# A two-layer kernel's attention: the diagonal of the scores in 32-token blocks, transposes moved to another ring, first loads spread over steps, and extra products in the first row phase

## The chip, the cores and the metric

The kernel runs on one core of a Trainium2 chip. The metric is the device time of one execution in microseconds. TensorE's granted clock has two levels here, 2.4 GHz (shown as 1.00) and 1.2 GHz (0.50).

## The reference

The whole program is two layers, each an attention followed by a mixture of experts. The change touches only the first attention: 2 sequences of 1024 tokens, 16 heads of 8 numbers each, keys and values rebuilt from a small latent.

```python
scores = jnp.einsum('bhqd,bhkd->bhqk', qh, kh) * scale
decay = jnp.exp(-LAMBDA_DECAY * TIME_STEP * jnp.abs(idx[:, None] - idx[None, :]))
scores = scores * decay[None, None, :, :]
attn = jax.nn.softmax(scores, axis=-1)
out = jnp.einsum('bhqk,bhkd->bhqd', attn, vh)
```

There is no causal mask. The decay exp(-c|i-j|) is a product of a factor of the query and a factor of the key, but a different product on each side of the diagonal: one pair of factors holds for keys before the query, another for keys after it.

## The kernel before, in words

Queries and keys are scaled with a ramp for each of the two sides ("half" 0 and 1 in the code), split into three bf16 parts, written to DRAM (parts_dram) and loaded back by load_side (L110, L113) into two big tiles, stack[0] and stack[1], four heads each. A pair of heads has two halves with a query side and a key side each, so four sides to load. Rows 72 to 74 of the stack carry the negated row maximum of each query, so that a product over 75 rows gives score minus maximum.

A head m has 8 key tiles t of 128 keys; a step is one (m, t), 256 steps in all. On TensorE one step of the main loop does, in program order:

- score_unit(m, t, 0) and (m, t, 1): scores of 128 keys against 512 queries each, into one of three PSUM banks used in turn (the score ring, NS = 3). Queries beyond the key tile use half 0, queries before it half 1, and the tile's own 128 queries use half 0. by_columns (L387) issues each product as four, one for each 32 keys, into the four column groups of the array.
- at t = 3 and 7, score_late (m, part): the 128x128 diagonal blocks of four tiles once more with half 1, 16 products of 128 columns.
- row_unit(n) for the row 15 steps ahead (LEAD): scores of 128 queries against 1024 keys into one of two row tiles (the row ring), of which DVE takes the maximum (L857).
- weigh(m, t - 2) (L501): probabilities times values, fp32, summed in out_ps; and at t = 7 and t = 1 or 2 weigh_late (L512) the same for the late blocks.
- turn_neg (L420) once in a head: a small transpose of the split maxima into the row ring. DVE copies it out (L867), and ACT's queue stores it into the stack (L627).
- turn_out (L446) once in four heads, at t = 4.

ACT does the exponentials (L641, L648). POOL zeroes the wrong triangle in each diagonal block (L768), and in the late blocks (L773), splits the maxima (L717 to L723), and in the first 12 steps prepares the second sequence's parts (L744, L752, L760). The order on each engine is the program order written here, and semaphores tie the engines together.

Before the main loop come the projections, and then 15 rows of the first phase (wide_row_unit, L412), 128 columns wide and with no scores between. After step 255 there are three tail steps, then the output copy.

## Time and the profile before

| what | value |
|---|---|
| median of 3 runs | 924.22 us (922.47 to 927.52) |
| profiled execution | 928.23 us, its span 926.8 us |
| TensorE busy | 762.0 us, 82% |
| DVE, ACT, POOL busy | 602.8, 481.3, 268.0 us |
| mean granted clock | 0.891 |

The first attention is the stretch from 0 to about 444 us. The rest of the program isn't touched.

### The profile page before, as it was taken

To read this page: it belongs to the slowest core of one execution; us is meant where nothing else is said; L and a number is where in the kernel's file an instruction comes from. 1 tells how busy PE (TensorE), PEld (TensorE's weight loads), DVE (VectorE), ACT (ScalarE), POOL (GpSimd) and SP (SyncE) were. 2 spreads that over 40 slices of the span, in tenths; PEclk is the share of its full clock that TensorE was granted. 3 is DMA by queue.
4 is the path that set the end of the run, shared out by engine and by line. 5 is a ranking of instruction groups with operands and counts; after the bars stand their busy time and mean duration, and the time that the engine had idled before them with its cause. 6 is when DMAs were issued, how large, how long until landed. Compare 5 with 4: busy or idle time off the path is not lost. (4 is left out here: it accounts for less than half of the span.)

```text
span 926.8 us, 26384 instructions
## 1 busy us (share of the span) xinstructions
PE 762.0 (82%) x10923; PEld 469.9 (51%) x10923; DVE 602.8 (65%) x1402; ACT 481.3 (52%) x966; POOL 268.0 (29%) x590
## 2 busy tenths in 40 slices
PE   6599999999999999998538949999995993128990
PEld 3246555555555555554416825666663561025770
DVE  3768888888888888883642134767677446753444
ACT  4748888787878888888214443334342322001222
POOL 2566434343334333435025522000000000015531
PEclk9759999999999999999758959999998996558995
DMA  5562411111111111000671128000000004001104
GB/s 169 164 152 101 123 55 55 53 55 47 54 55 55 54 55 44 4 4 3 190 221 41 34 80 277 2 1 1 2 1 1 1 0 137 3 6 39 39 26 145
DMA packets 40327, 59.13 MB, mean 64 GB/s; under 512 B 11108, under 2 KB 22061, under 8 KB 40208
## 3 DMA queue, kind: packets, MB, share of 16 engines
q1 hardware_dynamic: 35216, 50.09, 18.3%
q0 software_dynamic: 2304, 4.74, 2.0%
q10 hardware_dynamic: 2688, 2.61, 0.8%
q8 instruction: 87, 1.43, 0.6%
q14 instruction: 32, 0.26, 0.1%
HBM read 42.09 MB, written 15.07 MB: 62 GB/s over the span
## 5 line engine op out<-in xcount | busy, mean ns | idle before, releaser
L857 DVE CUSTOM_DVE_ANT_0 junk<-row,rest 128x1024 bf16<-128x1024 f32 x256 | 312.7, 1225 | 62.6 <-PE row L387 49.1
L641 ACT ACTIVATE prob<-score 128x512 f32<-128x512 f32 x512 | 274.3, 598 | 78.8 <-PE score L387 77.1
L387 PE MATMUL score<-stack 75*32 75x128 bf16 (+3 forms) x3840 | 179.3, 298 | 1.9 <-ACT prob L641 1.0
L501 PE MATMUL out_ps<-prob,v_aug 128*32 128x256 f32 x2048 | 156.6, 383 | 1.6 <-POOL prob L768 1.6
L387 PE MATMUL row<-stack 72*32 72x512 bf16 x1928 | 150.3, 387 | 0.7
L768 POOL TENSOR_SCALAR_AFFINE_SELECT prob<-prob 128x128 f32<-128x128 f32 x256 | 79.1, 309 | 192.5 <-ACT prob L641 187.6
L387 PEld LDWEIGHTS score<-stack 75*32 75x32 bf16 x3840 | 92.6, 97 | 65.4 <-ACT prob L641 16.7
L501 PEld LDWEIGHTS out_ps<-prob,v_aug 128*32 128x32 f32 x2048 | 62.9, 111 | 52.4 <-POOL prob L768 2.2
L1487 PE MATMUL up_ps<-rows_t,up_w 128*128 128x320 f32 (+1 forms) x192 | 62.0, 448 | 7.7 <-DVE rows_t L1699 5.0
L1773 POOL MEMSET ones<- 128x128 bf16 x2 | 0.4, 205 | 231.6 <-POOLq L1214 212.3
L387 PEld LDWEIGHTS row<-stack 72*32 72x32 bf16 x1928 | 48.6, 98 | 29.6 <-DVE top L857 5.2
L2006 PE MATMUL outs<-vm_w,mixed 128*64 128x256 f32 x512 | 61.7, 381 | 1.8 <-issue 1.8
L1786 POOL DMA_INDIRECT rows_in<-rows,owner x36 | 35.2, 978 | 69.4 <-DVE owner L1696 59.1
L2006 PEld LDWEIGHTS outs<-vm_w,mixed 128*64 128x64 f32 x512 | 41.9, 137 | 20.6 <-issue 8.1
L1798 POOL DMA_INDIRECT results<-rows_out,owner x36 | 35.8, 996 | 49.4 <-DVE rows_out L1713 41.6
L773 POOL TENSOR_SCALAR_AFFINE_SELECT prob_late<-prob_late 128x512 f32<-128x512 f32 x64 | 40.8, 637 | 26.7 <-ACT prob_late L648 26.7
L2090 ACT ACTIVATE squares<-outs 128x256 f32<-128x256 f32 x60 | 18.2, 389 | 57.4 <-PE outs L2006 57.4
L1559 ACT ACTIVATE acted<-up_ps 128x320 f32<-128x320 f32 x32 | 13.8, 437 | 61.6 <-PE up_ps L1487 42.5
L1487 PEld LDWEIGHTS up_ps<-rows_t,up_w 128*128 128x128 f32 x192 | 35.2, 206 | 19.0 <-issue 4.7
L648 ACT ACTIVATE prob_late<-score 128x512 f32<-128x512 f32 x64 | 39.0, 610 | 0.0
L2006 PEld LDWEIGHTS work<-h_t,a_w 128*64 128x64 f32 x512 | 29.1, 141 | 12.1 <-ACT mixed L2096 10.6
L1699 DVE COPY rows_t<-xturn_ps 128x256 f32<-128x256 f32 x18 | 7.6, 424 | 41.6 <-PE xturn_ps L1477 33.4
(305 smaller groups left out, 1076.1 us busy)
## 6 DMA issues: line engine op xcount, KB each, us to landing
stack<-parts_dram SPq DMA_DIRECT2D x32, 288.0 KB
stack<-parts_dram SPq DMA_DIRECT2D x96, 96.0 KB
parts_dram<-prob SPq DMA_DIRECT2D x12, 256.0 KB
parts_dram<-spare SPq DMA_DIRECT2D x12, 256.0 KB
results<-x_tok SPq DMA_DIRECT2D x12, 256.0 KB, 3.8
up_w<-in_L_ffn_w_dram SPq DMA_DIRECT2D x1, 2048.0 KB, 9.7
rows<-x_tok SPq DMA_DIRECT2D x8, 256.0 KB, 3.5
y<-results SPq DMA_DIRECT2D x8, 256.0 KB, 4.1
```

Source lines behind the costliest of these rows:

```text
L387: last = pe.matmul(out[c:c + 32, :], keys[:, c:c + 32], queries, start=True, stop=True)
L501: last = pe.matmul(out_ps[32 * c:32 * c + 32, h // 2 * (S // 4):(h // 2 + 1) * (S // 4)], v_aug[g % 3][:, t, h, :], moving[:, :, c, :], st ...
L641: act.activation(prob[:, t, w * HALF:(w + 1) * HALF], score[n % NS][:, :], ACT.Exp).then_inc(exped, 1)
L648: act.activation(prob_late[:, m % 2, w * HALF:(w + 1) * HALF], score[n % NS][:, :], ACT.Exp).then_inc(exped, 1)
L768: pool.affine_select(out=prob[:, t, at:at + P], in_=prob[:, t, at:at + P], compare_op=ALU.is_ge, fill=0.0, base=0, pattern=[[1, P]], chann ...
L773: pool.affine_select(out=prob_late[:, m % 2, of].rearrange("p (n c) -> p n c", c=P), in_=prob_late[:, m % 2, of].rearrange("p (n c) -> p n ...
L857: dve.tensor_tensor_reduce(junk[:, slot % 2, :], row[slot % 2][:, :], rest[:, S - P - t * P:2 * S - P - t * P], 1.0, LOWEST, ALU.mult, ALU ...
L1487: last = pe.matmul(up_ps[n % 2][j][:, 0:cap], w_up[:, j, e, c * P:(c + 1) * P], rows_t[:, e * cap:(e + 1) * cap], start=True, stop=True)
L1786: pool.indirect_dma_start(rows_in[:, t, :], None, rows[:, :], bass.IndirectOffsetOnAxis(owner[:, 1, t:t + 1], 0)).then_inc(r_in[t], 16)
L1798: pool.indirect_dma_start(results[:, :], bass.IndirectOffsetOnAxis(owner[:, 0, t:t + 1], 0), rows_out[:, t, :], None, bounds_check=K * T - ...
L2006: last = pe.matmul(out[c:c + HC], stationary[:, c:c + HC], moving, start=start, stop=stop)
L2090: last = act.activation(squares[:, 2 * k:2 * k + 2, :], outs[k][:, :, 0:D], ACT.Square)
```

## The change

- Diagonal blocks. In a key tile's own 128 queries, the products of each 32-key group are cut at that group's own 32 tokens: queries before them use half 1, after them half 0, and the 32x32 block itself half 0 with 32 more rows of the stack (KX to KM = 107 rows). Those rows hold a constant mask that adds a large negative number to the wrong triangle before the exponential. The mask is loaded by new DMAs (load_masks, four DMAs a call, one call on ACT's queue and three on SP's). Once in a head, at t = 0, score_late does the 32x32 blocks of all 8 tiles with half 1, 32 products of 32 columns.
- Late part. ACT takes one exponential of 256 columns in a head, in place of two of 512. POOL adds these blocks to prob, 8 adds of 32 partitions x 4 x 32 elements in a head (four after t = 3, four after t = 7). POOL's affine selects and weigh_late are gone.
- Lag. weigh runs 5 steps behind the scores, not 2; there are 5 tail steps, and OUT_AT is 7.
- Rings. turn_neg goes into the score ring, at t = 2, and ACT copies it out. From head 3 on SP's queue stores it.
- First loads. Pair 1's second half, pair 2 and later pairs are loaded at given steps.
- Extra products. keep_clock multiplies ident by 384 columns of x_t in fp32, and nothing reads the result: 12 before the first row unit, and one after each of the 15 row units of the first phase.

```diff
+            def keep_clock(out):
+                pe.matmul(out, ident[:, :], x_t[:, 0:WARM], start=True, stop=True)
             pe.wait_ge(ident_cast, 1)
+            for n in range(2):
+                pe.wait_ge(raw_copied[0, n], 2)
+            for n in range(WARM_FIRST):
+                keep_clock(row[1][:, 0:WARM])
+            pe.wait_ge(v_copied, 4)
             for step in range(-LEAD, 0):
                 for kind, n in slots_at(step):
...
+                    wide_row_unit(n)
+                    keep_clock(score[1 + n % 2][:, 0:WARM])
+                if step == NEG_0:
+                    turn_neg(0)
...
+                below, above = (lambda c: (1, begin, at + c, KX)), (lambda c: (0, at + c + SUB, end, KX))
+                if end <= at:
+                    pieces = [lambda c: (1, begin, end, KX)]
+                elif begin > at:
+                    pieces = [lambda c: (0, begin, end, KX)]
+                else:
+                    pieces = [below, lambda c: (0, at + c, at + c + SUB, KM), above]
+                for piece in pieces:
+                    for c in range(0, P, SUB):
+                        half, a, b, rows = piece(c)
+                        if a < b:
+                            last = pe.matmul(out[c:c + SUB, a - begin:b - begin], tile[0:rows, half, 1, h, at + c:at + c + SUB],
+                                             tile[0:rows, half, 0, h, a:b], start=True, stop=True)
+                last.then_inc(score_ready, 1)
...
+                for t in range(SB):
+                    for c in range(0, P, SUB):
+                        at = t * P + c
+                        last = pe.matmul(out[c:c + SUB, t * SUB:(t + 1) * SUB], tile[0:KM, 1, 1, h, at:at + SUB],
+                                         tile[0:KM, 1, 0, h, at:at + SUB], start=True, stop=True)
...
-                pe.wait_ge(masked, m * SB + t + 1)
-                pe.wait_ge(exped, unit(m, t, 1) + 1)
+                pe.wait_ge(added, 2 * GH * m + GH * (t // 4 + 1))
+                pe.wait_ge(score_read, unit(m, t, 1) + 1)
...
+                if t == NEG_AT and m + 1 < NH:
+                    turn_neg(m + 1)
...
+            act.wait_ge(rows_set, 1)
+            load_masks(act, 0, 0, masks_in[0])
...
                 if t % 4 == 3:
...
+                    pool.wait_ge(score_read, unit(m, t, w) + 1)
+                    for c in range(GH):
+                        begin, at = w * (4 * S - HALF), w * S + c * SUB
+                        of = slice(c * SUB, (c + 1) * SUB)
+                        own = prob_all[of, begin:begin + 4 * (S + P)].rearrange("p (t s) -> p t s", s=S + P)[:, :, at:at + SUB]
+                        late = prob_late[of, m % 2, 4 * w * SUB:4 * (w + 1) * SUB].rearrange("p (t s) -> p t s", s=SUB)
+                        pool.tensor_tensor(own, own, late, ALU.add).then_inc(added, 1)
```

## Rows read from the trace of the kernel before

**Rows 1.** The page: granted clock in 40 slices of 23.2 us, in tenths.
```profile
PEclk9759999999999999999758959999998996558995
```

**Rows 2.** Stretches: length, busy us (count) of PE, PEld, DVE, ACT, POOL, clock, DMA share, GB/s.
```profile
19.00:27.40 8.40, 7.69 (x44) 5.37 (x42) 6.87 (x7) 6.71 (x10) 0.00 (x0) 1.00 0.39 117
...
35.20:54.00 18.80, 15.39 (x35) 2.43 (x39) 16.61 (x28) 6.09 (x8) 14.83 (x12) 0.50 0.50 162
54.00:70.00 16.00, 16.00 (x186) 9.38 (x189) 8.82 (x17) 10.32 (x20) 10.34 (x18) 0.50 0.78 166
...
200.00:250.00 50.00, 49.81 (x1136) 28.68 (x1132) 42.90 (x75) 40.87 (x78) 18.54 (x60) 1.00 0.18 51
```

**Rows 3.** Timeline, TensorE at the end of a head: start, duration, work, count.
```profile
201.28 0.83 PE L387 MATMUL score<-stack 75*32 75x512 bf16 x28
...
201.94 0.61 PE L387 MATMUL row<-stack 72*32 72x512 bf16 x8
...
202.38 0.61 PE L501 MATMUL out_ps<-prob,v_aug 128*32 128x256 f32 x8
202.81 0.39 PE L512 MATMUL out_ps<-prob_late,v_aug 128*32 128x128 f32 x8
203.03 0.61 PE L387 MATMUL score<-stack 75*32 75x512 bf16 x8
```

**Rows 4.** Timeline, where heads 13, 14, 2 and 30 begin (t = 0).
```profile
215.91 0.61 PE L387 MATMUL score<-stack 75*32 75x512 bf16 x8
...
227.42 0.39 PE L387 MATMUL score<-stack 75*32 75x512 bf16 x4
...
84.40 0.39 PE L387 MATMUL score<-stack 75*32 75x512 bf16 x4
...
417.23 0.61 PE L387 MATMUL score<-stack 75*32 75x512 bf16 x8
```

**Rows 5.** Timeline, the step after the small transpose: its scores, then its row unit.
```profile
409.84 0.88 PE L387 MATMUL score<-stack 75*32 75x384 bf16 x28
...
410.70 0.62 PE L387 MATMUL row<-stack 72*32 72x512 bf16 x8
```

**Rows 6.** Groups by form: count, busy us, mean ns of one, idle before.
```profile
L857 DVE CUSTOM_DVE_ANT_0 junk<-row,rest 128x1024 bf16<-128x1024 f32 x226 | 276.6, 1225 | 53.6 <-PE row L387 45.7
...
L719 POOL TENSOR_TENSOR top_left<-top,neg_parts 128x8 f32<-128x8 f32 x28 | 5.6, 202 | 2.4
...
L752 POOL TENSOR_TENSOR spare<-spare 128x512 f32<-128x512 f32 x4 | 4.7, 1170 | 0.0
...
L1779 POOL TENSOR_TENSOR share<-weight 128x128 f32<-128x128 f32 x1 | 0.4, 399 | 10.3 <-DVEq L1637 10.3
```

**Rows 7.** Timeline of the start: ACT's table load and first copy, first row unit.
```profile
4.89 1.28 ACT L556 ACT_TABLE_LOAD   x1 [4.89 <-issue]
...
7.46 0.59 ACT L556 COPY x_t<-score 128x512 f32<-128x512 f32 x1 [1.29 <-PE score L345]
...
35.22 1.87 PE L412 MATMUL row<-stack 72*128 72x512 bf16 x4 [7.79 <-issue]
```

**Rows 8.** Timeline, end of the first phase, and the starts of heads 0 and 1.
```profile
47.37 4.20 POOL L707 TENSOR_TENSOR spare<-spare 128x1024 bf16<-128x1024 f32 x2
...
49.34 1.23 DVE L857 CUSTOM_DVE_ANT_0 junk<-row,rest 128x1024 bf16<-128x1024 f32 x1 [1.00 <-PE row L412]
...
53.96 1.04 PE L387 MATMUL score<-stack 75*32 75x512 bf16 x8
...
72.13 0.61 PE L387 MATMUL score<-stack 75*32 75x512 bf16 x7
```

**Rows 9.** Timeline of the attention's end.
```profile
422.32 3.97 POOL L768 TENSOR_SCALAR_AFFINE_SELECT prob<-prob 128x128 f32<-128x128 f32 x1 [1.12 <-ACT prob L641]
...
438.11 0.72 ACT L648 ACTIVATE prob_late<-score 128x512 f32<-128x512 f32 x1
...
440.08 0.59 ACT L659 COPY o_t<-out_ps 128x512 f32<-128x512 f32 x1 [1.25 <-PE out_ps L512]
```

More of the change, by code:

```diff
@@ L54, in host_constants @@
     before = (p[:, None] < p[None, :]).astype(np.float32)
+    r, col = np.arange(SUB)[:, None], np.arange(S)[None, :] % SUB
+    low = np.where(np.stack([col < r, col >= r], 1), 0xC700, 0)
+    one = np.stack([col == r, col == r], 1) * 0x3F80
+    mask = np.stack([low, one], 2).astype(np.uint16).view(np.int32)
     return {
         "c_ramp": np.ascontiguousarray(np.broadcast_to(ramp[None], (P, 2, S))),
-        "c_bound": bound, "c_rest": rest, "c_ident": ident, "c_before": before,
+        "c_bound": bound, "c_rest": rest, "c_ident": ident, "c_before": before, "c_mask": mask,
         "c_causal": (p[:, None] % HC <= np.arange(HC)[None, :]).astype(np.float32),
@@ L302, in _, with after, fill_side @@
             sp.wait_ge(stored[0], FILL * 16)
-            for pair in range(2):
-                for side in range(2):
-                    load_side(sp, dram, stack[0], pair, 1, side, stacks_in[1][pair])
-            def fill_side(pair, n, units):
+            for side in range(2):
+                load_side(sp, dram, stack[0], 0, 1, side, stacks_in[1][0])
+            def after(step):
+                sp.wait_ge(score_ready, unit(step // SB, step % SB, 0) + 1)
+            def fill_side(pair, n, step):
@@ L309, in fill_side @@
                 half, side = n // 2, n % 2
-                if units:
-                    sp.wait_ge(scored, units)
+                after(step)
                 load_side(sp, dram, stack[pair // 2 % 2], pair, half, side, stacks_in[half][pair % 4])
+            for n in range(2, 4):
+                fill_side(1, n, 0)
+            load_masks(sp, 0, 2, masks_in[1])
             sp.wait_ge(rows_set, 2)
             for n in range(4):
-                fill_side(2, n, 0)
-            for n in range(4):
-                fill_side(3, n, 0)
+                fill_side(2, n, (6, 8, 10, 13)[n])
@@ new lines, in _ @@
+            after(15)
+            load_masks(sp, 1, 0, masks_in[2])
+            fill_side(3, 0, 16)
+            store_neg(sp, 3)
+            for n in range(1, 4):
+                fill_side(3, n, (19, 21, 23)[n - 1])
+            store_neg(sp, 4)
+            after(27)
+            load_masks(sp, 1, 2, masks_in[3])
+            for n in range(2):
+                fill_side(4, n, 28 + 2 * n)
+            fill_side(4, 2, 32)
+            store_neg(sp, 5)
+            fill_side(4, 3, 36)
+            for n in range(2):
+                fill_side(5, n, 38 + 2 * n)
@@ L319, in _ @@
+            store_neg(sp, 6)
+            for n in range(2, 4):
+                fill_side(5, n, 39 + 2 * n)
             for k in range(FILL):
                 store_parts(sp, 1, 0, k // NPART, k % NPART, stored[1])
-            for pair in range(1, PAIRS):
-                if pair == 2:
+            for pair in range(6, PAIRS + 3):
+                first = (pair - 3) * 2 * SB
+                if pair == 8:
+                    sp.wait_ge(stored[1], 2 * FILL * 16)
+                for n in range(4):
+                    if n in (2, 3):
+                        m = 2 * (pair - 3) + n - 1
+                        if n == 3 and pair < PAIRS:
+                            fill_side(pair, 2, first + 6)
+                        if m < NH:
+                            store_neg(sp, m)
+                    if n != 2 and pair < PAIRS:
+                        fill_side(pair, n, first + (0, 1, 6, 10)[n])
+                if pair == 6:
+                    after(60)
@@ L468, in score_unit @@
                     pe.wait_ge(stacks_in[1][m // 2 % 4], (m // 8 + 1) * LOADS * 16)
+                    if m < 2 * GH and m % 2 == 0:
+                        pe.wait_ge(masks_in[m // 2], 64)
                     pe.wait_ge(neg_in[m % 2], (m // 2 + 1) * 32)
                 out = free_score(unit(m, t, part))
-                for half, a, b in ((1, begin, min(end, at)), (0, max(begin, at), end)):
-                    if a < b:
-                        last = by_columns(out[:, a - begin:b - begin], tile[0:KX, half, 1, h, at:at + P],
-                                          tile[0:KX, half, 0, h, a:b])
@@ L527, in _ @@
                     row_unit(slots.pop(0)[1])
-                for kind, head, n in weighs_at(step):
-                    if kind == "tile":
-                        weigh(head, n)
-                    else:
-                        weigh_late(head, n)
+                for head, n in weighs_at(step):
+                    weigh(head, n)
+                if t == NEG_AT and m + 1 < NH:
+                    turn_neg(m + 1)
                 for kind, n in slots:
-                    if kind == "neg":
-                        turn_neg(n)
-                    elif kind == "out":
+                    if kind == "out":
                         turn_out(n)
```

203 lines of the change are left out of this document (99 added, 104 removed).

## The prediction

> **What bounds the kernel now.** I first read the clock line of the page: full clock nearly everywhere up to slice 19, but half in the second and third slices [rows 1]. The stretches say where: full from 19 to 27.4 us, half from 35.2 to 70, full again in the middle [rows 2]. In the middle TensorE is busy 49.81 of 50 us, while DVE has 42.90, ACT 40.87 and POOL 18.54 [rows 2]. So in the main loop TensorE's program is the time, and each product taken out of it counts, until DVE's 1.225 us for a row unit [rows 6] binds. A step of the loop is two score sets, two row sets (0.44 us, 201.94 to 202.38) and a weigh (0.43), 1.31 in all [rows 3], so DVE is not far behind.
>
> In the half-clock stretch from 54 to 70 TensorE is busy all the time [rows 2], so there it is bound by its clock: head 0 takes 72.13 - 53.96 = 18.2 us [rows 8], where head 13 takes 227.42 - 215.91 = 11.51 [rows 4]. A head that leads a group of four takes 215.91 - 203.03 = 12.88 [rows 3, 4]. The first phase (35.2 to 54) is DVE's: 16.61 busy of 18.8 [rows 2].
>
> **Main loop, part by part.** Removed from each head: two score_late units of 0.22 each (201.28 to 201.94 is 0.66, of which two ordinary sets are 0.44) and two weigh_late of 0.22 (202.81 to 203.03) [rows 3]: 0.88. The small transpose leaves the row ring. Now the row unit behind it starts 410.70 - 409.84 = 0.86 after its scores [rows 5], where 0.66 is the work [rows 3]: it waits 0.20 for DVE, which also has the transpose to copy. With that gone: 1.08 a head. In the score ring the transpose's bank is asked for again only a step later, and ACT, which copies it, has 9 of 50 us free [rows 2].
>
> Added: one unit of 32 products of 32 columns. Streaming alone is 8 x 32 columns a column group, half of the 512 of a 0.22 set: 0.11. At the densest rate that the trace shows for pairs of weight load and product (16 in 0.22, or 0.0139 us each [rows 3]) it is 0.44. I take the middle, 0.28. Further, each own-diagonal unit has three sets of unequal lengths in place of one or two, still 512 columns for each group. If products start in program order, the third set can't start before the last group has finished its first and begun its second; the first group then idles up to 96 columns less its own 32, some 0.03 us. The bounds are 0 and one more 128-column set, 0.22/4 = 0.055. I take 0.03, eight times a head: 0.24. So a head saves 1.08 - 0.28 - 0.24 = 0.56. A leading head now costs 1.37 more than others; turn_out's own products are no more than about half of that, and the rest is waiting in the row ring, of which I give back half, 0.35. A group of four: 4 x 0.56 + 0.35 = 2.6; heads 2 to 29 are seven groups, 18.2 us.
>
> The Trainium skill speaks against this (TensorE: Matmul & The Clock Gate, section "Wait — 56ns, not 53.3ns?"): start-to-start never drops below about 25 ns, however few the columns. By that rule the late unit would be 0.8 us and the head slower than before. Here 16 products start within 0.22 us, four column groups side by side, so for these products the floor doesn't hold as stated; whether it holds at 32 columns no row shows.
>
> **The new wait for POOL.** weigh now waits for the adds, and behind it stand, in program order, all later scores; ACT waits for those. Price of an add of 128 elements a lane: a 128x128 add took 0.399 [rows 6]; between 8 and 512 elements (0.202 and 1.170) a straight line gives 0.43. Strides and 32 partitions are not seen in it. Four take 1.7. In a steady head the exponentials of t = 3 end about 1.05 us after its scores begin, the adds at 2.8 to 3.0, and weigh(m, 0) stands 2 x 1.33 + 0.87 = 3.5 behind: 0.5 free. For t = 7 it is 1.6 + 1.8 = 3.4 against 1.33 + 0.28 + 1.33 + 0.87 = 3.8, 0.4 free. So nothing is charged; without that cover each 0.1 us of an add costs 0.8 a head less the free time. POOL's total doesn't grow: 8 x 0.43 replace ten selects. ACT loses two 512-column exponentials and DMA issues, and gains one short one and a small copy. SP's queue gets store_neg. Its maxima are ready at the end of t = 2 and needed 5 steps (6.6 us) later; a fill is issued a step or more earlier, so I charge nothing.
>
> **The start.** Four mask DMAs stand on ACT's queue ahead of its 1.28 us table load [rows 7]. If each takes about the 0.45 of its neighbours, the load starts at 6.7 rather than 4.89 and the first copy (7.46) at 8.0. I charge 0.5, with bounds 0 and 2.5. The other mask and stack loads have several steps each before they are read.
>
> **The extra products.** A weigh, fp32 and 256 columns in each column group, takes 0.43, so 384 columns in fp32 are 0.64 at full clock. TensorE is idle for 7.79 us before 35.22 [rows 7]; twelve take 7.7 there. Between row units 0.64 stands beside a row's 0.43: 1.07, under DVE's 1.2. At full clock they are therefore hidden. From 19 to 27.4, with TensorE on fp32 products over the whole array, the clock was full [rows 2]; it was half after the idle 7.79 us. I take it that with the idle time filled the clock stays full to the main loop.
>
> **First two heads.** In the first phase the transpose's slot goes: DVE waited 1.00 and copied 0.2 before 49.34 [rows 8]. Step 0 starts at 53.96 - 1.2 + 0.5 = 53.3. TensorE alone would then need 0.3 + 5 x 1.2 (no weighs yet, DVE's pace) + 3 x 1.33 + 11.0 and be at head 2 at 74.6, not 84.40 [rows 4]. But POOL is late next: free at 51.6 [rows 8], it has until t = 7 of head 1 twelve part operations of 1.17, sixteen adds of 0.43 and two splits of 1.1, 23.1 us, and first waits about 2.3 for row 15's maximum. That is 77, and its splits and adds hold TensorE at several places; stepping through the two programs by these prices I get head 2 at 78.8. Gain 5.6 (bounds: 0, and 9.8).
>
> **The end.** Before, 440.08 - 417.23 = 22.85 us from head 30 to the output copy [rows 4, 9]. After: without row units ACT sets the pace, 40.87/78 = 0.52 an exponential [rows 2], so 16 steps of 1.05 and two short ones, 17.5. One POOL operation took 3.97 us while DVE ran its reach reductions [rows 9]; the adds of t = 3 will meet them too, some 2 us. After the last exponential come 1.7 of adds, four weighs of 0.43 and hand-overs, 3.8, where 1.25 stood before. Sum 23.3: 0.5 lost.
>
> **Sum.** 18.2 + 5.6 - 0.5 = 23.3 saved. From the profiled execution's 928.2 that is 905; it lay 4 us over the median of 924.2, from which it is **901 us**.
>
> **Rivals.**
> - Small sets fill a whole slot: late unit 0.44, diagonal 8 x 0.055 = 0.44. A head saves 0.20, a group 1.15, seven groups 8; with 5.1 from the ends, 911 us. For it: every set in the trace starts only when the one before has streamed, and weights must be loaded between. Against it: nothing that forces 32 columns to cost 128. 16 in 100.
> - Another engine takes over (DVE's row, 1.225 of a step of 1.34, or ACT), or the ring waits stay, and only the first heads gain: 917. 10 in 100.
> - The clock is not held, so the change doesn't do what it says: the twelve end at 27.4 + 15.4 = 42.8, not 35.2 (7.6 lost), and a row unit with its extra product is 2.15, not 1.2 (14 lost); the early gain goes. 924.2 - 18.2 + 0.5 + 21.6 = 928. Against it the 19 to 27.4 row. 7 in 100.
> - The other side: POOL's adds are too slow and each weigh waits. At 0.8 us an add, 3.2 for four, a head waits about 2 x 1.0 and the 28 heads lose 2.0 - 0.6, 40 us: 960. It decides from about 0.6 us an add, where four overrun their cover by 0.3. Against it 0.399 [rows 6]. 6 in 100.
> - TensorE can't issue so many: 1136 products in 50 us [rows 2] were 22.7 a us; a head now has 285 (265 before) in 11 us, 26 a us. If 22.7 is a ceiling, a head takes 12.5 and the kernel about 945. Against it the 28 products within 0.66 us [rows 3]. 3 in 100.
>
> The forecast itself gets 58 in 100, and alone would lie in 889 to 911 (late unit 0.11 to 0.44, diagonals 0 to 0.44, early gain 2 to 9). The range, 889 to 919, takes in the first two rivals. Half a per cent, 4.6 us, is about what a measurement here can tell. Faster by more: 58 + 16 + 9 = 83; slower by more: 10; within: 7.
>
> **What would show it.** The clock line full from the first slices on; head 2 at about 79; heads of 10.95 us, leaders 12.0; a late unit of 0.28; the own-diagonal units 0.03 over 0.22; POOL adds at 0.43, and no wait of out_ps for POOL in the middle; TensorE still busy over 97% there. Wrong it would be if the waits list shows weigh behind POOL, if the clock shows 0.50 between 35 and 50, or if heads stay at 11.4.

## The result, and the profile after

The changed kernel takes **913.19 us** (median of 4 runs, 910.09 to 914.89); beside it the kernel before took 923.35 (919.42 to 927.52). The ratio is 0.9886, with a 95% interval of 0.9848 to 0.9925: 10.2 us saved, where 23.3 had been worked out. The time lies within the forecast range of 889 to 919, and the change made the kernel faster, but by less than half of what was forecast. The profiled execution took 912.28 us, with a span of 910.7.

I read the clock line first, as for [rows 1]. Columns are 40 slices of 22.8 us, in tenths of full clock:

```profile
PEclk9978997999999999998858959999998996558995
```

Full almost from the start, but there are dips in the third and fourth slices, in the seventh, and near the end of the attention (slice 19). The stretches that answer to [rows 2], with the same columns, say how deep they are:

```profile
35.20:54.00 18.80, 17.60 (x155) 8.13 (x153) 17.52 (x31) 7.00 (x12) 14.33 (x16) 1.00 0.41 123
54.00:60.00 6.00, 4.00 (x71) 1.71 (x75) 3.75 (x8) 3.96 (x9) 5.62 (x9) 0.77 0.66 142
60.00:76.00 16.00, 16.00 (x253) 8.09 (x249) 8.10 (x13) 10.64 (x21) 10.86 (x18) 0.55 0.20 58
100.00:138.00 38.00, 37.13 (x933) 23.17 (x922) 33.56 (x56) 30.73 (x61) 14.09 (x38) 1.00 0.48 136
138.00:153.00 15.00, 13.64 (x206) 7.72 (x210) 6.41 (x11) 5.96 (x12) 4.01 (x12) 0.54 0.15 38
...
200.00:250.00 50.00, 49.89 (x1303) 30.51 (x1299) 44.93 (x75) 41.59 (x83) 20.73 (x58) 1.00 0.22 59
```

The first phase has its full clock (1.00 against 0.50 in [rows 2]), so the products do what was expected of them. It is lost just behind that phase (0.77, 0.55) and once more at 138, in the middle of the attention (0.54), where the kernel before had it full. The undisturbed middle is TensorE's alone: 49.89 of 50 us.

The timeline of TensorE (start, duration, work, count) around head 13's and 14's first steps answers to [rows 3] and [rows 5]:

```profile
201.28 0.64 PE L554 MATMUL score<-stack 107*32 107x32 bf16 x15
201.72 0.44 PE L565 MATMUL score<-stack 107*32 107x32 bf16 x32
202.00 0.63 PE L448 MATMUL row<-stack 72*32 72x512 bf16 x8
202.43 0.62 PE L583 MATMUL out_ps<-prob,v_aug 128*32 128x256 f32 x8
202.87 0.64 PE L554 MATMUL score<-stack 75*32 75x128 bf16 x16
203.32 0.62 PE L448 MATMUL row<-stack 72*32 72x512 bf16 x8
...
205.51 0.73 PE L554 MATMUL score<-stack 75*32 75x416 bf16 x15
206.07 0.61 PE L448 MATMUL row<-stack 72*32 72x512 bf16 x8
```

The late unit starts at 201.72 and the row unit behind it at 202.00: 0.28. A pair of own-diagonal units takes 201.72 - 201.28 = 0.44 or 203.32 - 202.87 = 0.45, so the third set costs 0.01, not 0.03. The row unit of the step with the small transpose starts 0.56 after the scores, where [rows 5] have 0.86: it no longer waits. But the transpose itself still takes 0.56 - 0.44 = 0.12 of TensorE's time there.

The groups of the main loop (100 to 400 us; mean ns of one) answer to [rows 6]:

```profile
L851 POOL TENSOR_TENSOR prob<-prob,prob_late 32x128 f32<-32x128 f32 x208 | 93.9, 452 | 160.1 <-ACT prob L713 148.4
L791 POOL TENSOR_TENSOR top_left<-top,neg_parts 128x8 f32<-128x8 f32 x26 | 5.2, 202 | 2.1
```

An add is 0.452 against the 0.43 of the forecast, and in the list of waits TensorE has in that stretch no wait of a weigh for an add.

**Where the attention's time went.** Head 2 begins at 80.86, head 30 at 402.95, and the output turns at 432.94:

```profile
32.48 0.60 PE L473 MATMUL row<-stack 72*128 72x512 bf16 x2
...
80.86 0.63 PE L554 MATMUL score<-stack 107*32 107x32 bf16 x15
...
402.95 0.64 PE L554 MATMUL score<-stack 107*32 107x32 bf16 x15
...
432.94 0.63 PE L522 MATMUL row<-ident,o_t 128*128 128x128 f32 x4 [0.80 <-ACT o_t L731]
```

Against [rows 4]: head 2 is 84.40 - 80.86 = 3.5 us earlier (forecast 5.6), although this execution began its row units 2.7 us sooner than [rows 7]. The 28 heads between take 402.95 - 80.86 = 322.1, where [rows 4] give 332.8 and the forecast 314.6: 7.5 missing. And the end takes 30.0, where the kernel before had 440.81 (its turn of the output) - 417.23 = 23.6 and the forecast 24.1: 5.9 missing. Together the output turns 7.9 us sooner, not 23.3. What follows the attention is the same code; it took 486.0 us in the profiled execution before and 477.8 after (span less the turn of the output), and 475 to 481 in those of the experiments up to e12, so that the 8.2 us between the two profiles there are no gain of the change. The main loop itself is as forecast where nothing disturbs it; the loss lies at three places.

**At 50 to 60 us**, TensorE's timeline (in brackets the idle time before, and what ended it):

```profile
50.39 0.63 PE L554 MATMUL score<-stack 75*32 75x32 bf16 x15 [0.88 <-DMA stack<-neg_rows]
...
54.23 0.22 PE L487 MATMUL score<-ident_b,neg_parts 128*24 128x128 bf16 x1 [0.51 <-ACT prob L713]
...
56.52 0.41 PE L554 MATMUL score<-stack 75*32 75x32 bf16 x11 [0.73 <-ACT prob L713]
...
58.81 0.62 PE L554 MATMUL score<-stack 75*32 75x128 bf16 x12 [0.98 <-ACT prob L713]
59.22 1.07 PE L448 MATMUL row<-stack 72*32 72x512 bf16 x8
```

The first line's bracket names the store of the maxima; the load of the stack that the first score also needs had landed 0.6 us before it (49.62 and 50.25 in the trace's semaphore events). The last line, 1.07 for eight products that take 0.61 elsewhere, is at half clock: the clock fell at 57.2 and came back at 74.3. ACT's own timeline shows it in the casts of the part rows, which wait for POOL.

```profile
53.05 0.65 ACT L683 CAST spare<-spare 128x512 bf16<-128x512 f32 x1
53.56 1.13 ACT L713 ACTIVATE prob<-score 128x512 f32<-128x512 f32 x2
54.53 0.24 ACT L699 COPY neg_rows<-score 24x128 bf16<-24x128 bf16 x1
55.35 0.62 ACT L683 CAST spare<-spare 128x512 bf16<-128x512 f32 x1 [0.58 <-POOL spare L816]
...
60.04 0.62 ACT L683 CAST spare<-spare 128x512 bf16<-128x512 f32 x1 [0.79 <-POOL spare L816]
```

**At 137.6**, head 7. TensorE, then SP's queue:

```profile
136.87 0.71 PE L583 MATMUL out_ps<-prob,v_aug 128*32 128x256 f32 x8
139.36 1.05 PE L554 MATMUL score<-stack 75*32 75x32 bf16 x15 [1.79 <-issue]
```

```profile
123.44 6.43 SPq L294 DMA_DIRECT2D parts_dram<-spare  x6
129.92 1.25 SPq L114 DMA_DIRECT2D stack<-parts_dram  x1
131.21 2.09 SPq L117 DMA_DIRECT2D stack<-parts_dram  x3
133.35 1.58 SPq L301 DMA_DIRECT2D stack<-neg_rows  x2
```

"issue" is idle time that the view puts down to nothing; in the trace's semaphore events TensorE stands there 2.40 us on the semaphore of head 7's maxima (neg_in). Their store, two transfers of 6 KB, was issued at 133.35, behind six part stores of 256 KB each and four loads. Behind the wait the clock is half from 139.1 to 152.8. Two ordinary heads take 21.9 us; heads 6 and 7 take 30.8 together, so that 9.0 are lost here, of which TensorE is idle for 2.1 (1.79, and 0.34 in the middle of a row unit at 136.7).

**At 406.6**, POOL's splits for head 31, with DVE's reach reductions beside them, and TensorE behind:

```profile
405.70 1.18 POOL L789 CAST neg_parts<-top 128x8 bf16<-128x8 f32 x1 [0.36 <-DVE top L943]
406.95 1.07 POOL L791 TENSOR_TENSOR top_left<-top,neg_parts 128x8 f32<-128x8 f32 x1
...
409.24 1.07 POOL L795 TENSOR_TENSOR neg_parts<-top_left,neg_parts 128x8 bf16<-128x8 f32 x1
```

```profile
405.60 1.23 DVE L976 CUSTOM_DVE_ANT_0 junk<-y 128x1024 bf16<-128x1024 f32 x1
...
406.75 1.22 DVE L976 CUSTOM_DVE_ANT_0 junk<-y 128x1024 bf16<-128x1024 f32 x1
```

```profile
410.46 0.27 PE L487 MATMUL score<-ident_b,neg_parts 128*24 128x128 bf16 x1 [3.55 <-POOL neg_parts L795]
```

Four operations that take 0.20 each in the middle take 1.07 to 1.18, each as long as the reduction beside it. TensorE waits 3.55, and the clock is half from 408.8 to 415.6. The Trainium skill (SBUF — State Buffer, section "Who interferes with whom") says that a DVE instruction with two SBUF inputs contends with a GpSimd instruction that reads SBUF. A reach reduction has both its inputs in SBUF, and the durations agree.

### The profile page after: what moved, and what is told of

Read it like the earlier page. It is cut to its first block and busy times, and to the rows that moved or that the text cites. A ratio compares the mean times of both kernels' runs of the same rounds, so it can differ in the third digit from the quotient of the medians.

```text
span 910.7 us, 27734 instructions
## 1 busy us (share of the span) xinstructions
PE 756.4 (83%) x11617; PEld 483.1 (53%) x11617; DVE 598.9 (66%) x1370; ACT 469.4 (52%) x966; POOL 270.0 (30%) x526
## 5 line engine op out<-in xcount | busy, mean ns | idle before, releaser
L554 PE MATMUL score<-stack 75*32 75x512 bf16 (+14 forms) x3968 | 174.1, 283 | 5.2 <-issue 1.8
L851 POOL TENSOR_TENSOR prob<-prob,prob_late 32x128 f32<-32x128 f32 x256 | 115.5, 451 | 190.1 <-ACT prob L713 175.6
L583 PE MATMUL out_ps<-prob,v_aug 128*32 128x256 f32 x2048 | 162.8, 393 | 3.9 <-POOL prob L851 3.9
L448 PE MATMUL row<-stack 72*32 72x512 bf16 x1928 | 154.4, 391 | 0.3 <-issue 0.3
L554 PEld LDWEIGHTS score<-stack 75*32 75x32 bf16 (+1 forms) x3968 | 106.9, 98 | 74.5 <-ACT prob L713 10.4
L583 PEld LDWEIGHTS out_ps<-prob,v_aug 128*32 128x32 f32 x2048 | 65.9, 113 | 55.2 <-POOL prob L851 11.1
L448 PEld LDWEIGHTS row<-stack 72*32 72x32 bf16 x1928 | 53.4, 97 | 12.5 <-issue 2.0
L1859 POOL DMA_INDIRECT rows_in<-rows,owner x36 | 35.2, 977 | 69.7 <-DVE owner L1769 59.4
L2163 ACT ACTIVATE squares<-outs 128x256 f32<-128x256 f32 x60 | 18.2, 389 | 57.4 <-PE outs L2079 57.4
L2079 PEld LDWEIGHTS work<-h_t,a_w 128*64 128x64 f32 x512 | 29.3, 142 | 12.1 <-ACT mixed L2169 10.6
L2079 PE MATMUL work<-h_t,a_w 128*64 128x128 f32 x512 | 33.3, 285 | 1.0 <-PEq L1412 0.9
L2169 ACT COPY mixed<-work 128x512 f32<-128x512 f32 x32 | 18.7, 586 | 25.7 <-PE work L2079 20.9
L2214 DVE TENSOR_REDUCE heads_sum<-heads 128x128 f32<-128x1024 f32 x16 | 31.2, 1949 | 0.5
```

The source lines that it names most:

```text
L448: last = pe.matmul(out[c:c + 32, :], keys[:, c:c + 32], queries, start=True, stop=True)
L554: last = pe.matmul(out[c:c + SUB, a - begin:b - begin], tile[0:rows, half, 1, h, at + c:at + c + SUB], tile[0:rows, half, 0, h, a:b], star ...
L583: last = pe.matmul(out_ps[32 * c:32 * c + 32, h // 2 * (S // 4):(h // 2 + 1) * (S // 4)], v_aug[g % 3][:, t, h, :], moving[:, :, c, :], st ...
L851: pool.tensor_tensor(own, own, late, ALU.add).then_inc(added, 1)
L1859: pool.indirect_dma_start(rows_in[:, t, :], None, rows[:, :], bass.IndirectOffsetOnAxis(owner[:, 1, t:t + 1], 0)).then_inc(r_in[t], 16)
L2079: last = pe.matmul(out[c:c + HC], stationary[:, c:c + HC], moving, start=start, stop=stop)
```

## The experiments

Each edit is made to the changed kernel unless it says otherwise, and each ratio is against the kernel before, run on the same chip between them. One table holds what the traces show of the attention: the first row unit, head 2's begin, the 28 heads from 2 to 29, from head 30 to the turn of the output, and when that turn starts, all in us. Begins of heads are taken 0.70 before the row unit behind their late unit.

| kernel | first row unit | head 2 | 28 heads | end | output turns |
|---|---|---|---|---|---|
| before | 35.2 | 84.4 | 332.8 | 23.6 | 440.8 |
| before, with products | 34.8 | 84.1 | 332.2 | 23.6 | 439.8 |
| forecast | 35.2 | 78.8 | 314.6 | 24.1 | 417.5 |
| changed | 32.5 | 80.9 | 322.1 | 30.0 | 432.9 |
| changed, run again (e11) | 36.3 | 81.3 | 323.7 | 29.9 | 434.9 |
| e1, store of head 7 on ACT | 34.6 | 81.5 | 315.1 | 30.2 | 426.7 |
| e2, fill in steps 0 to 4 | 34.8 | 88.2 | 316.4 | 29.6 | 434.1 |
| e3, reach spread | 35.1 | 84.1 | 317.3 | 26.6 | 428.1 |
| e4, no products | 34.4 | 81.2 | 317.6 | 29.2 | 428.0 |
| e5, load order | 35.1 | 80.0 | 320.6 | 29.3 | 429.8 |
| e6, e1 + e3 + e5 | 35.1 | 81.1 | 317.0 | 26.4 | 424.5 |
| e7, e6, no products | 35.2 | 81.2 | 321.5 | 26.8 | 429.4 |
| e9, e6 + casts later | 36.0 | 79.5 | 316.9 | 25.2 | 421.6 |
| e10, e9 + fill | 34.9 | 78.1 | 316.8 | 26.7 | 421.6 |
| e12, e9, no products | 35.1 | 81.7 | 321.2 | 25.2 | 428.0 |
| e13, stores spread | 35.0 | 81.0 | 314.0 | 30.2 | 425.2 |
| e14, e3 + e5 + casts later + e13 | 35.0 | 78.6 | 314.7 | 25.7 | 419.0 |

### Head 7's maxima on another queue

Theory: SP's queue is in order, and the store waits there behind the part stores and fills.

```diff
 # SP
-                        if m < NH:
+                        if m < NH and m != 7:
                             store_neg(sp, m)
 # ACT
-                if t == 4 and m < 2:
+                if t == 4 and m in (0, 1, 6):
                     store_neg(act, m + 1)
```

> The changed kernel, with head 7's negated maxima stored by ACT's queue (as heads 1 and 2 are) instead of SP's, where they stood behind six stores of parts (6.43 us of issuing) and two fills. Theory A (the store was late in SP's queue, TensorE waited 1.79 us at head 7, and the clock then fell to half for 13.7 us): the wait at 137.6 us is gone, the clock stays full from about 75 us to 400, head 7 takes 10.9 and not 16.8 us, and the kernel is about 9 us faster than the changed one, so near 904. Rival B (the clock falls at this place for another reason, or the transfer itself is late behind the bulk stores whatever queue issues it): the wait or the half-clock stretch stays, gain under 2 us. Without any wait but with a clock that falls by itself: 2 to 3 us.

Measured: 908.86 us, ratio 0.9894 (0.9827 to 0.9960). The 28 heads fall from 322.1 to 315.1, and the clock is no longer half there:

```profile
100.00:138.00 38.00, 37.20 (x938) 22.24 (x931) 33.29 (x57) 31.16 (x61) 13.61 (x38) 1.00 0.50 140
138.00:153.00 15.00, 14.91 (x409) 9.14 (x409) 13.00 (x21) 11.66 (x23) 6.90 (x21) 1.00 0.31 90
```

But a wait for the maxima stays, 0.70 us on their semaphore, though ACT issues the store at 131.33, 2.0 earlier than SP did. From the first issue to the head's first score are 7.4 us (131.33 to 138.70), where the changed kernel has 6.0 (133.35 to 139.36): issued earlier on another queue, the maxima were longer under way. So the order of the queue was at most part of it. The ratio of the whole does not tell this kernel from the changed one. Nor is the fall of the 28 heads this edit's for certain: e2, e3 and e4 below store as the changed kernel does and wait as long (2.31, 1.33 and 2.11 idle), but there the clock stays full (e4: half for 3.4 us), and their 28 heads take 316.4 to 317.6.

### A product in the steps without a weigh

```diff
                 if slots and slots[0][0] == "row":
                     row_unit(slots.pop(0)[1])
+                if step < WEIGH_LAG:
+                    pe.matmul(out_ps[:, 0:192], ident[:, :], x_t[:, 0:192], start=True, stop=True)
```

Nobody reads these products either; they stand where a weigh will stand from step 5 on, and TensorE has less to do.

> The changed kernel, with one more product that nobody reads (fp32, 192 columns, 0.32 us at full clock) after the row unit in each of steps 0 to 4, the steps without a weigh. Theory A (in those steps TensorE has too little to do, which lets the clock fall at 57.2 us for 17 us): the clock stays full, and head 2 starts at 76 to 78.5, where POOL's chain holds it, rather than 80.95; kernel 2.5 to 5 us faster. Rival B (the clock fell because of the waits of 0.5 to 1.0 us for ACT, which waited for POOL): it falls all the same, no change within 1 us, or up to 1 us slower by the added products.

Measured: 913.67 (10 runs), 0.9925 (0.9885 to 0.9965). It failed: TensorE waited 3.36 us for its data ahead of the first score (load and maxima, the maxima last), the clock was half from 56.9 to 73.9 all the same, four of the five extra products ran at half clock, and head 2 began at 88.2. That wait is not the edit's, which stands behind it: with the same code ahead of the first score it was 0.88 in the changed kernel, 1.86 in e1 and 2.51 in e3. So e2 says little of what the products would do without it; e10 does.

### The reach reductions one at a time

```diff
+REACH_AT = (133, 141, 149, 157)
 # DVE, main loop, behind the row of step
+                        if step in REACH_AT:
+                            k = REACH_AT.index(step)
+                            dve.wait_ge(row_done, slot_at["row", n] + 1)
+                            reach(k // 2, k % 2)
+                            dve.wait_ge(reached, k + 1)
...
 # DVE, behind the last row
-                        dve.wait_ge(row_done, slot_at["verdict", 0])
-                        for b in range(B):
-                            for side in range(2):
-                                reach(b, side)
```

> The changed kernel, with DVE's four reach reductions done one at a time at steps 133, 141, 149 and 157 in place of all four after the last row unit. Theory A (two-input DVE operations hold up POOL's maxima split, TensorE waits 3.55 us at head 31's transpose, and its clock is half from 408.8 to 415.6): the wait is gone, from head 30 to the output's transpose takes 24 to 25 us and not 29.9, kernel 5 to 6 us faster. Rival B (the wait moves to something else, the ring or the adds): under 2 us.

Measured: 909.11, 0.9882 (0.9815 to 0.9949). The splits are back at their usual length, and the end takes 26.6 instead of 30.0:

```profile
404.21 0.19 POOL L790 CAST neg_parts<-top 128x8 bf16<-128x8 f32 x1 [0.36 <-DVE top L944]
404.49 0.20 POOL L792 TENSOR_TENSOR top_left<-top,neg_parts 128x8 f32<-128x8 f32 x1
404.75 0.19 POOL L794 CAST neg_parts<-top_left 128x8 bf16<-128x8 f32 x1
405.02 0.20 POOL L796 TENSOR_TENSOR neg_parts<-top_left,neg_parts 128x8 bf16<-128x8 f32 x1
```

The 3.55 us wait and the half clock behind it are gone. The end is not down to the 24 to 25 expected: what stays are TensorE's four waits for POOL's adds, 0.64, 0.72, 0.71 and 2.25. And the reductions now cost something in the middle, where DVE has little time free: heads 16 to 20 take 1.4 us more than in the changed kernel (58.0 against 56.6), so that 2.0 of the 3.4 are net.

### The change without its products

```diff
-            for n in range(WARM_FIRST):
-                keep_clock(row[1][:, 0:WARM])
...
-                    keep_clock(score[1 + n % 2][:, 0:WARM])
```

> The changed kernel without any of the 27 extra products. Theory A (they keep the clock up in the first phase, which is paced by DVE anyway): the clock falls at about 32 us and is half until about 70; the first phase itself is no longer, but heads 0 and 1 are slower; kernel 1 to 4 us slower than the changed one, little because the clock falls at 57 us anyway. Rival B (the products are worth the whole early gain): 6 us or more slower. Rival C (they cost more than they give): faster.

Measured: 909.84, 0.9880 (0.9819 to 0.9942), no slower than with them. The first phase is at half clock, and yet no longer:

```profile
35.20:54.00 18.80, 16.21 (x85) 2.90 (x87) 17.76 (x30) 7.21 (x11) 16.00 (x13) 0.50 0.43 130
```

From the first row unit to head 2 are 46.8 us, between the 48.4 and 45.0 of the changed kernel's two profiles (the second is e11). DVE sets the pace of that phase with either clock (17.76 and 17.52 busy of 18.8), and the clock that the products hold is lost at 57.2 (62.5 in e11) in any case.

### The load ahead of head 0

The load of pair 1's first half stood on SP's queue ahead of pair 0's second-half loads.

```diff
             for side in range(2):
                 load_side(sp, dram, stack[0], 0, 0, side, stacks_in[0][0])
-            for side in range(2):
-                load_side(sp, dram, stack[0], 1, 0, side, stacks_in[0][1])
             for side in range(2):
                 for k in range(NPART):
                     store_parts(sp, 0, 1, side, k, stored[0])
+            for side in range(2):
+                load_side(sp, dram, stack[0], 1, 0, side, stacks_in[0][1])
```

> The changed kernel, with the load of pair 1's first half moved on SP's queue from ahead of the six stores of the second half's parts to behind them. Theory A (head 0's first scores wait for the chain stores, landing, load of pair 0's second half, so that the extra products and the freed ring slot only bring TensorE sooner to that wait of 0.9 to 3.4 us): from the first row unit to the first score it takes 16 to 17 us and not 18 to 20.5, the wait is gone or under 1 us, and the clock doesn't fall at 55 to 57 us; head 2 is reached 2 to 6 us earlier after the first row unit than in the changed kernel's runs (47.6 to 54). Rival B (the wait is for ACT's store of the negated maxima): no change of the first score's time. Rival C (the clock falls anyway, because TensorE has little to do in steps 0 to 4): the first score comes earlier, but the clock is still half for 17 us from about 55.

Measured: 909.40, 0.9825 (0.9794 to 0.9856). The wait for a DMA ahead of the first score is gone. The score starts 17.0 us after the first row unit, as expected (17.9 and 17.3 in the changed kernel's two profiles, 18.9 to 20.4 in e1, e2 and e3), and head 2 starts 44.9 after it, which the changed kernel reaches in one of its two profiles as well (48.4 and 45.0). The maxima, which landed last before, are quicker too: 3.4 us from the first issue to landing, where the changed kernel has 4.8 and e2 7.1. The waits behind ACT stay, and the clock still falls, for 10 us, where the two profiles of the changed kernel have 17 and 7:

```profile
58.16 0.41 PE L554 MATMUL score<-stack 75*32 75x32 bf16 x11 [0.72 <-ACT prob L713]
60.45 0.62 PE L554 MATMUL score<-stack 75*32 75x128 bf16 x12 [1.22 <-ACT prob L713]
```

### The three together, with and without products

No new lines: e6 is e1 + e3 + e5, and e7 is e6 without the 27 products.

> The changed kernel with the three repairs together: head 7's store on ACT's queue, DVE's reach reductions spread, the load order. Theory A (the three losses are separate): attention ends (the output's last transpose) near 418 to 424 us, against 432.9 in the changed kernel's profile and 440.8 before; median 900 to 905. Rival B (one wait gives way to the next): 907 or more.

> The same three repairs without the 27 extra products. Theory A (the products pay once TensorE needn't wait for its first scores, because the clock then stays full into the main loop): 3 to 7 us slower than with them, the clock half from 31 to 69 us. Rival B (POOL's chain sets when head 2 starts, with or without the clock): within 2 us of it.

Measured: 906.44 (0.9802, 0.9773 to 0.9830) and 907.79 (0.9810, 0.9778 to 0.9842). e6 lies between the bounds of its two theories (905 and 907). Its output turns at 424.5, sooner than with any one of the three (426.7, 428.1, 429.8), but they do not simply add up: the 28 heads take 317.0, of which 1.4 are the spread reductions', and 2.5 are still lost at heads 6 and 7 (24.3 us together). The products are still worth nothing that shows: head 2 comes 46.0 us after the first row unit in both.

### The products alone, in the kernel before

```diff
+            def keep_clock(out):
+                pe.matmul(out, ident[:, :], x_t[:, 0:384], start=True, stop=True)
+            for n in range(12):
+                keep_clock(row[1][:, 0:384])
...
+                        keep_clock(score[1 + n % 2][:, 0:384])
```

> The kernel before, with the 27 extra products alone. Theory A (there the main loop follows with weighs from step 2 and TensorE fully busy, so a clock that is full at 54 us stays full): half clock from 32 to 70 us is gone, head 0 takes 11 to 14 us and not 18.2, the kernel 4 to 7 us faster than before. Rival B (the clock falls at 55 us all the same): within 2 us.

Measured: 923.36 (10 runs), ratio 1.0011 (0.9970 to 1.0051). The clock is full to 54 and it is worth nothing:

```profile
35.20:54.00 18.80, 16.64 (x60) 7.72 (x59) 17.47 (x31) 5.90 (x8) 14.66 (x12) 1.00 0.54 155
54.00:70.00 16.00, 15.27 (x193) 8.88 (x197) 7.77 (x14) 10.04 (x19) 10.28 (x17) 0.57 0.77 170
```

TensorE waits 2.01 us for a DMA ahead of the first score, the clock falls at 55.0, and head 2 starts at 84.1, where it started at 84.4 [rows 4].

### The casts of the part rows later

```diff
-                if 1 <= step < 5:
-                    late_first_part(step - 1)
+                if 4 <= step < 8:
+                    late_first_part(step - 4)
```

> The three repairs together, and ACT's four casts of the second sequence's parts moved from steps 1 to 4 to steps 4 to 7. Theory A (in steps 2 to 4 ACT stands in those casts waiting for POOL, TensorE waits for ACT 0.5, 0.7 and 1.2 us, and its clock falls just then, at 59.3 us): the waits of TensorE for ACT before 60 us are gone or under 0.3 us, and the clock stays full; head 2 is reached 2 to 4 us earlier than with the three repairs alone (81.8 us there). Rival B (the clock falls because TensorE has little to do without weighs): the waits go, the clock falls at 55 to 60 us all the same. Rival C (POOL's own chain sets head 2): head 2 moves by less than 1 us.

Measured, with e6's edits: 903.37 (900.77 to 905.25), 0.9801 (0.9754 to 0.9849). Head 2 comes 43.6 us after the first row unit, just the 78.8 - 35.2 of the forecast, and the end takes 25.2. Of TensorE's three waits for ACT two are left (0.50 and 0.73), so the casts stood behind the third alone (1.21 in e6); the clock is half for 10.2 us, from 59.5.

> The same, and a product that nobody reads (fp32, 192 columns) in each of steps 0 to 4. Theory A: no further change, within 1 us. Rival B (little to do in these steps lets the clock fall): only now does the clock stay full through 50 to 75 us. Rival C (POOL's chain sets head 2): the clock may stay full, head 2 moves by less than 1 us against the version without the product, and the waits turn up as TensorE waiting for POOL.

Measured (e9 with e2's product): 905.48, 0.9825 (0.9777 to 0.9873). With no wait ahead of the first score the five products do hold the clock: it is full from 17.7 to 417. The two waits for ACT before 60 us are gone with them, so whether it was these waits or the little work in the steps without a weigh that let the clock fall, no run tells; they come together.

```profile
60.00:76.00 16.00, 13.71 (x337) 7.34 (x333) 11.75 (x20) 13.84 (x30) 14.62 (x22) 1.00 0.31 84
```

Yet only 0.4 us is gained up to head 2 (43.2 against 43.6): TensorE idles 2.3 of these 16 us instead, most of it for POOL (0.97 for the splits, 0.43 for the adds), which has 14.62 of them busy. Behind the clock stood POOL, as the forecast had said for this stretch.

### The changed kernel again, and e9 without products

> The changed kernel itself, unchanged, beside the others on the same chip, for the spread. If its profile's half clock from 139 to 153 us was an accident of one execution on top of a wait that is always there, the wait of 1.3 to 2.3 us at head 7 is here again and the half-clock stretch behind it need not be; median 910 to 914.

> The best version so far (three repairs, later casts; 903.4 us, 0.980 of the kernel before) without the 27 extra products. Theory A (with the waits gone the products carry a full clock into the main loop): the clock is half from about 32 to 66 us, head 2 is reached 2 us or more later after the first row unit than the 44.3 us with them, median 905.5 or more. Rival B (POOL's chain sets when head 2 starts, so the products are worth nothing): 45 us or less, median within 1.5 us of 903.4.

The changed kernel, on the chip of e9: 915.09 (12 runs), 0.9934 (0.9900 to 0.9967), with the same three losses (0.71 and 1.22 for ACT at 60; 3.8 idle and half clock from 141.0 to 154.7; 3.56 for POOL at 409). So between kernels run side by side e9 is 1.3% faster than the changed one. e12: 905.54, 0.9860 (0.9813 to 0.9908). Without products head 2 comes 46.5 us after the first row unit, with them 43.6. So with the wait ahead of the first score gone and the casts later they are worth 2.9 us there, in one profile of each; the ratios of the whole, 0.9801 and 0.9860, have intervals that overlap. e12 also lost 4 us at head 7, to be seen next.

### The part stores spread

In e12 ACT issued head 7's maxima at 131.63, and TensorE still waited 4.26 us on them, to 141.1; in e7 4.58, in e9 0.78. Counted from the start of the first issue to head 7's first score that is 6.0 us in the changed kernel and 5.1 to 7.2 in e2 to e5 and e11 (SP's queue), and 7.4, 7.7, 9.5 and 10.2 in e1, e9, e12 and e7 (ACT's): the earlier issue on ACT's queue brings the maxima in hardly sooner. Rival to the queue's order: the part stores, 1.5 MB at once, and the fills behind them occupy the DMA engines. Then they must be spread, and the maxima may stay on SP. The kernel before speaks for it. It issues the same six stores, at 97 us, and has its maxima on ACT's queue:

```profile
97.15 6.33 SPq L278 DMA_DIRECT2D parts_dram<-spare  x6
101.01 0.73 ACTq L627 DMA_DIRECT2D stack<-neg_rows  x1
```

These maxima landed at 107.10 (semaphore events), 6.1 us after their issue, where those issued at 126.13 took 2.8; TensorE did not need them yet. The price was there to read, hidden by slack.

```diff
             store_neg(sp, 4)
+            for k in range(0, 2):
+                store_parts(sp, 1, 0, k // NPART, k % NPART, stored[1])
...
             store_neg(sp, 5)
+            for k in range(2, 4):
+                store_parts(sp, 1, 0, k // NPART, k % NPART, stored[1])
...
             store_neg(sp, 6)
+            for k in range(4, 6):
+                store_parts(sp, 1, 0, k // NPART, k % NPART, stored[1])
...
-            for k in range(FILL):
-                store_parts(sp, 1, 0, k // NPART, k % NPART, stored[1])
```

> The changed kernel, with the six stores of the second sequence's first parts (256 KB each) issued two at a time behind the stores of the maxima of heads 4, 5 and 6, rather than all six behind step 45. Theory A (TensorE waits at head 7 for its maxima because they land behind 1.5 MB of stores and 0.6 MB of loads): the wait for the maxima at head 7 is gone (0.05 us as at other heads), no half clock between 100 and 400 us, heads 2 to 29 take 313 to 316 us; median 3 to 9 us under the changed kernel's 913 to 915. Rival B (something else at this place): wait and half clock stay. Rival C (the collision moves to heads 4 to 6): waits of 0.5 us or more there.

> Stores spread, load order, reach reductions spread and casts later, together, with the extra products; the maxima's queue as in the change. Theory A (separate losses): head 2 about 44.3 us after the first row unit, 28 heads in 313 to 316, end as with the spread reductions (24 to 26 us from head 30 to the output's transpose): attention ends near 419 to 422, median 900 to 903. Rival B (they overlap): no better than 903.4.

Measured: 919.71 for e13, beside 929.92 for the kernel before on this slower chip, ratio 0.9882 (0.9841 to 0.9922). The stretch that held the stall is whole:

```profile
100.00:138.00 38.00, 37.89 (x988) 24.23 (x985) 34.03 (x58) 31.29 (x62) 13.77 (x38) 1.00 0.60 144
138.00:153.00 15.00, 15.00 (x384) 10.06 (x383) 13.31 (x23) 12.72 (x26) 6.92 (x21) 1.00 0.32 96
```

The 28 heads take 314.0 us, where the forecast had 314.6, with the maxima still on SP's queue: they land 4.7 us after their issue, in time. Heads 6 and 7 take 22.1 together. The bulk transfers were the cause. What in their path holds the small ones stays open: from 123 to 139 us the DMA engines of the changed kernel are 0.52 to 0.68 busy in the mean, not full, and in e13 no less up to 131. e14, all four edits in one, has head 2 at 78.6, the heads in 314.7 and the turn of the output at 419.0, where the forecast had 417.5. Its time is 912.62 (907.49 to 915.52) beside 929.92 (behind the attention, where the code is the same, its profiled execution took 486.9 us and e13's 492.5, so whether it would reach the expected 900 to 903 elsewhere isn't shown): **0.9809** (0.9772 to 0.9847). e5, e6, e7, e9, e10 and e14 lie at 0.980 to 0.983 with intervals that overlap, and no run tells them apart; only e9 and e10 ran side by side with the changed kernel.

## Why the prediction was right and wrong

- **Main loop, right, in part by luck.** 28 heads 18.2 us shorter was the sum; 18.8 and 18.1 were measured (e13, e14: 332.8 - 314.0 and 332.8 - 314.7). Late unit 0.28 and forecast 0.28, by chance of the middle: the unit took under two thirds of the 0.44 that the densest rate in the trace before gave. Heads are 10.93 and leaders 11.93 (10.95 and 12.0), but two errors of like size cancel there. The own-diagonal units cost 0.01 each, some 0.1 a head and not 0.24. And of the 0.20 at the small transpose only 0.08 was DVE's wait: the rest, 0.12, is the transpose's own work, which stays. The adds took 0.452, not 0.43, hidden as said. The rivals of small sets that fill a slot (911), of slow adds (960), of another engine (917, though 924.2 - 5.1 makes 919) and of an issue ceiling (945; 1303 products in 50 us are 26.1 a us) are refuted by these numbers.
- **"I charge nothing" for the maxima in SP's queue, wrong.** This is the step that cost most: 7.5 us in the changed kernel, 9.1 when it ran again (323.7 - 314.6). I counted that a fill is issued a step before, and did not look for what else is issued there: six stores of 256 KB once in the kernel, behind which two transfers of 6 KB took 5.9 us to land (133.35 to 139.27) in place of the 2.7 of the head before (119.61 to 122.33). The wait itself is 2.40; the rest is the half clock that follows it. How much follows is chance as far as the runs show: with the same stores on the same queue 1.8 to 3.0 us are missing in e2, e3 and e4, 6.0 in e5. Spreading the stores gives all of it back (e13); the other queue doesn't (0.5 missing in e1, 6.6 in e12).
- **The end, "0.5 lost", undersized: 6.4 lost.** The clue stood in [rows 9], an operation of POOL stretched to 3.97 under DVE's reductions. I priced it for the adds, some 2 us, and not for the four splits that now stand between the reductions and TensorE. Spreading the reductions returns 3.4 of it (e3). The wait of the last weigh for the adds, 2.25, was in the sum; the three before it, 0.64, 0.72 and 0.71, were not. Without row units weighs stand closer behind the adds, and the sum took ACT's pace alone.
- **The early gain, 5.6, undersized in the changed kernel** (3.5, of which 2.7 is an earlier start of this execution; in e11 3.1, with a start 1.0 later). The bound named, POOL's chain at 78.8, fits: with load order and casts mended head 2 comes at 79.5 and 78.6. Missing was who waits for POOL: ACT, in order, with its casts ahead of exponentials, and with ACT TensorE (one wait of three). Also missing were the transfers ahead of the first score, for which TensorE waited 0.88 and 0.29 in the changed kernel's two profiles, and up to 3.36 in e2.
- **"I take it that with the idle time filled the clock stays full to the main loop", half right.** It stayed full to 57.2 (62.5 in e11), and fell behind waits of 0.5 to 1.2 us in steps with little work; kept full to the end in e10, it was worth 0.4 us, since POOL was next. The rival that the clock is not held (928) is refuted for the first phase, but its reverse was missing from the list: that it is held and worth nothing, as e4 against the changed kernel and e8 against the kernel before show (1.0011).
- **The start, 0.5 for four mask DMAs.** Four took 1.90 on ACT's queue, and the first copy began at 8.08, not 7.46: 0.6.

Still open: why the clock fell behind some waits and not behind others of like length; why the wait on head 7's maxima ranged from 0.70 to 4.58 us between kernels that store them alike; what stops TensorE in the middle of a row unit just ahead of the stores' wait, where its program has none (0.34 in the changed kernel, 0.91 in e11); and what the four waits for adds that are left at the end would give back, which wasn't tried.

## What to carry to other kernels

Before a small transfer is moved into a queue and costed at nothing, list everything that this queue and the DMA engines carry in the steps around it, the rare bulk moves first: an average share of 0.18 says nothing of the one place with 1.5 MB. When a wait is removed, follow the next one through every in-order engine; here POOL's lateness reached TensorE through casts on ACT. When a sum comes out right, check its parts too: here two errors of 0.12 and 0.14 a head cancelled. A clock held by idle products is worth only what TensorE bounds in that stretch, so work out that bound before adding them.

## What the runs showed of the hardware

- 32 products of 32 columns, eight in each of four column groups, took 0.26 to 0.28 us in all: 35 ns for each set of four side by side, 8.8 ns from one start to the next. By the floor of about 25 ns in the Trainium skill (TensorE: Matmul & The Clock Gate, section "Wait — 56ns, not 53.3ns?") these 32 would need 0.8, an estimate. The trace doesn't agree across column groups; within one group, at 35 ns, it doesn't contradict the floor.
- A store of two transfers of 6 KB let its reader go 5.1 to 7.2 us after its issue on the queue of 1.5 MB of stores and 0.6 MB of loads, and 7.4 to 10.2 on another queue beside them; with little else under way it lands in 2.7 to 2.8.
- POOL's 0.20 us operations on 8 elements took 1.07 to 1.18 each while DVE ran its reductions of 1.22 back to back: one for one.
- Behind a wait of 1.8 us at full clock TensorE ran 13.7 us at half (changed kernel at 139), and 13.7 again behind 0.9 and 2.9 (e11), but only 3.4 behind 3.45 (e7), and not at all behind 0.7 (e1) or 2.31 (e2). In the changed kernel the half clock cost more than the wait: 9.0 us lost with 2.1 idle.
